# K and V of each context chunk: eight block products replaced by seven shared ones (Strassen, one level)

## The reference, cut to what matters

```
q = proj(layernorm(x), Wq, bq);  k = proj(ctx, Wk, bk);  v = proj(ctx, Wv, bv)   # [256|25088, 512] x [512, 512]
scores = q @ k.T / sqrt(64)         # per head of 64 columns, 2 sequence halves of the context
out = softmax(scores) @ v           # x + out goes on
```

## Time and profile before

| | us |
|---|---|
| median of 3 runs (1722.69 to 1724.3) | 1722.85 |
| profiled execution, its own time | 1723.75 |
| its span, first to last instruction | 1722.0 |
| PE busy / DVE / ACT / POOL in the span | 1661.5 / 1090.8 / 1095.7 / 365.8 |

### The profile page before, as it was taken

The page is one execution under the profiler, slowest core; times in us unless marked ns, Lnnn a source line. Parts: engine busy times, 40 slices in busy tenths (PEclk is TensorE's granted clock), DMA queues, the critical chain, the costliest instruction groups (busy, mean ns, idle before and its releaser), DMA issues.

```text
span 1722.0 us, 38963 instructions
## 1 busy us (share of the span) xinstructions
PE 1661.5 (96%) x14196; PEld 930.2 (54%) x14196; DVE 1090.8 (63%) x1559; ACT 1095.7 (64%) x2775; POOL 365.8 (21%) x500
## 2 busy tenths in 40 slices
PE   6999999999999999999999999999999587999998
PEld 3455555555555555555555555555555365777776
DVE  4666666666666666666666666666666556676765
ACT  3676676766766667666676666666666435555554
POOL 3222222222222222222222222322222100000000
PEclk9999999999999999999999999999999775999999
DMA  6466554555545555455554655545554470465551
GB/s 239 83 127 124 108 122 103 128 122 110 122 100 131 119 112 123 97 134 113 114 126 97 133 106 120 128 97 130 106 122 83 81 251 1 148 214 189 207 195 50
DMA packets 442396, 215.93 MB, mean 125 GB/s; under 512 B 416736, under 2 KB 422880, under 8 KB 435568
## 3 DMA queue, kind: packets, MB, share of 16 engines
q1 hardware_dynamic: 442064, 215.07, 51.6%
q10 hardware_dynamic: 288, 0.27, 0.1%
HBM read 111.96 MB, written 0.56 MB: 65 GB/s over the span
## 4 chain that ended last, share of the span: by engine, by line
PE 94%; DVE 2%; ACT 1%; DMA 1%; issue 1%; POOL 0%; SPq 0%; DVEq 0%; ACTq 0%; POOLq 0%
PE ps_proj L828 60%; PE ps_proj L948 9%; PE ps_s L845 9%; PE ps_o L864 8%; PE ps_o L971 4%; PE ps_s L904 1%; PE ps_proj L884 1%; PE ps_proj L915 1%; DVE wsp L655 1%; DMA ctx_f<-ctxt_dram 1%; PE ps_o L891 0%; PE ps_o L807 0%; ACT prob L390 0%; POOL ctx_s L306 0%; DVE cmax L584 0%
## 5 line engine op out<-in xcount | busy, mean ns | idle before, releaser
L828 PE MATMUL ps_proj<-ctx_s,wk_s 128*128 128x512 f16 x2352 | 542.1, 381 | 9.4 <-POOL ctx_s L306 9.4
L828 PE MATMUL ps_proj<-wv_s,ctx_s 128*128 128x512 f16 x2352 | 540.2, 379 | 0.0
L390 ACT ACTIVATE prob<-ps_s,nmax 128x256 f32<-128x256 f32 x784 | 360.5, 471 | 231.5 <-DVE nmax L591 231.5
L306 POOL TENSOR_TENSOR ctx_s<-ctx_f,ctx_s 128x512 f16<-128x512 f32 x196 | 230.6, 1177 | 908.8 <-ACT ctx_s L355 908.8
L828 PEld LDWEIGHTS ps_proj<-ctx_s,wk_s 128*128 128x128 f16 x2352 | 216.2, 98 | 264.7 <-issue 23.9
L828 PEld LDWEIGHTS ps_proj<-wv_s,ctx_s 128*128 128x128 f16 x2352 | 215.4, 98 | 252.7 <-issue 20.3
L573 DVE SCALAR_TENSOR_TENSOR k_s<-ps_proj,bk_s,k_s 128x512 f16<-128x512 f32 x196 | 147.1, 751 | 222.7 <-ACT k_s L362 222.7
L610 DVE SCALAR_TENSOR_TENSOR p_s<-prob,p_s 128x1024 f16<-128x1024 f32 x196 | 240.2, 1226 | 55.1 <-ACT p_s L401 55.1
L584 DVE TENSOR_REDUCE cmax<-ps_s 128x4 f32<-128x1024 f32 x196 | 239.1, 1220 | 25.7 <-PE ps_s L845 25.6
L576 DVE TENSOR_TENSOR v_s<-ps_proj,v_s 128x512 f16<-128x512 f32 x196 | 134.5, 686 | 186.5 <-ACT v_s L364 186.5
L401 ACT ACTIVATE p_s<-prob 128x1024 f16<-128x1024 f32 x196 | 210.4, 1073 | 0.1
(11 more groups left out here) (118 smaller groups left out, 904.1 us busy)
## 6 DMA issues: line engine op xcount, KB each, us to landing
ctx_f<-ctxt_dram SPq DMA_DIRECT2D x49, 1024.0 KB, 5.1
wst<-w_dram SPq DMA_DIRECT2D x96, 512.0 KB, 4.2
pt_s<-p_s SPq DMA_TRANSPOSE x392, 3.2
w_in_sb<-w_in_dram SPq DMA_DIRECT2D x1, 3072.0 KB, 11.6
tisa<-tisa_scores SPq DMA_DIRECT2D x3, 1024.0 KB, 14.1
w_f<-wk_dram SPq DMA_DIRECT2D x1, 1024.0 KB, 7.9
w_f<-wv_dram SPq DMA_DIRECT2D x1, 1024.0 KB, 11.9
w_f<-wq_dram SPq DMA_DIRECT2D x1, 1024.0 KB, 13.6
```

The lines of the kernel that those rows point to most:

```text
L306: pool.tensor_tensor(out=ctx_s[odd][1][:, t, :], in0=ctx_f[odd][:, t, :], in1=ctx_s[odd][0][:, t, :], op=ALU.subtract).then_inc(ctx_low, 1)
L390: ins = act.activation(prob[:, g % 2, (2 * b + r) * HC:(2 * b + r + 1) * HC], ps_s[:, b, r * HC:(r + 1) * HC], ACT.Exp, bias=nmax[odd][:, ...
L828: ins = pe.matmul(ps_proj[:, u % 4, :], lhsT, rhs, start=(t == 0 and n == 0), stop=(t == DT - 1 and n == 2))
```

## The change

With a chunk's context as a 2 x 2 of blocks b11, b12, b21, b22 (256 input features x 256 rows each) and the weight likewise, K and V each take seven block products (Winograd's form) in place of eight. The pieces are:

- Context: four sums t1 to t4 (fp32, 512 elements a partition each) on POOL, then high and low parts of seven blocks in place of four. ACT writes the high parts of three blocks (one instruction of 1024, one of 512 elements), POOL copies the high parts of the four sums (two of 1024) and writes all low parts (three of 1024, one of 512).
- Weights: the same sums once, at the start, for K on DVE and for V on POOL, with their high and low parts; chunk 0's low parts on DVE.
- PE: `unit` is 12 matmuls of 256 columns (before: 12 of 512), 14 units a chunk (before: 8). They are M1, M5, M6, M2, M7, M3, M4 for K (first half of a step, h = 0) and again for V (h = 1), laid around the scores of two groups and two weightings.
- Shared products are combined in PSUM: ACT copies M1's bank into a second one (`seed`), on which M6 accumulates; ACT copies M5 to SBUF (`copy_m5`); DVE adds it (`add_u4`, then `add_c22`). Four output blocks for K and four for V are then split as before (`block_highs` on ACT, `block_lows` on DVE).
- `step` has two halves instead of four groups. In it the high and low part of an odd group's probabilities go to the next half. The load of `w_in_sb` moves from the start to step 47, into memory that the context's buffers leave; `tisa_scores` and `project_q` change places at the start.

The core of the diff:

```
-            def project(c, odd, u):
...
+            def unit(k, odd, h, m):
+                w, x, role = m
+                g, first = 2 * k + h, isinstance(k, int) and k == 0
...
+                if m == M1:
+                    if h == 0 and not first:
+                        pe.wait_ge(ctx_low, DT * (k + 1))
+                    if not isinstance(k, int) or g >= 1:
+                        pe.wait_ge(block_low, 4 * g - 3)
+                elif m == M5:
+                        pe.wait_ge(block_low, 4 * g - 2)
+                elif m == M6:
+                    pe.wait_ge(seeded, g + 1)
+                elif m == M7:
+                    pe.wait_ge(u4_done, g + 1)
+                elif m == M4:
+                    pe.wait_ge(c22_done, g + 1)
+                for sub in range(2):
+                    for t in range(2):
+                        for i, (a, b) in enumerate(THREE):
...
+            def step(c, odd):                                 # PE
+                for h in range(2):
+                    for half, before, between, behind in ((0, (M1,), (M5, M6), (M2, M7)), (1, (), (M3,), (M4,))):
+                        g = 2 * h + half
+                        units(*before)
+                        if exists(c, 0):
+                            scores(c, g, odd)
+                        units(*between)
+                        vc, vg = back(c, g, PV_LAG)
+                        if exists(vc, 0):
+                            weigh(vc, vg, odd if g >= PV_LAG else 1 - odd)
+                        units(*behind)
...
+            def step(c, odd):                                 # ACT
+                for h in range(2):
+                    if exists(c, h):
+                        block_highs(c + h, 1 - h, C21, odd if h == 0 else 1 - odd)
+                    if exists(c, 1):
+                        seed(c + 1, h)
+                    pc, pg = back(c, 2 * h, 1)
+                    if exists(pc, 0):
+                        p_highs(pc, pg)
...
+                    if exists(c, 1):
+                        copy_m5(c + 1, h)
+                    if exists(c, 0):
+                        exps(c, 2 * h, odd)
                     if exists(c, 2):
+                        ctx_highs(c + 2, odd, h)
...
+                        p_highs(c, 2 * h)
                     if exists(c, 1):
+                        for which in (C11, C22, C12):
+                            block_highs(c + 1, h, which, 1 - odd)
                     if exists(c, 0):
+                        exps(c, 2 * h + 1, odd)
...
             def step(c, odd):                                 # DVE
+                for h in range(2):
+                    if exists(c, h):
+                        block_lows(c + h, 1 - h, C21, odd if h == 0 else 1 - odd)
                     if exists(c, 0):
+                        maxima(c, 2 * h, odd)
...
+                        p_lows(pc, pg)
                     if exists(c, 1):
+                        add_u4(c + 1, h)
+                    if exists(c, -1):
+                        add_o(c - 1, h)
                     if exists(c, 0):
+                        p_lows(c, 2 * h)
+                    if exists(c, 1):
+                        add_c22(c + 1, h)
+                    if exists(c, 0):
+                        maxima(c, 2 * h + 1, odd)
+                        step_max(c, h, odd)
+                    if exists(c, 1):
+                        for which in (C11, C22, C12):
+                            block_lows(c + 1, h, which, 1 - odd)
...
+            def add_c22(k, h):
+
+                g = 2 * k + h
+                dve.wait_ge(unit_done, UNITS * g + 5)
+                dve.tensor_tensor(half_bank(bank(h, 3)), half_bank(bank(h, 1)), m5_f[:, :, :], ALU.add).then_inc(c22_done, 1)
...
-            def ctx_lows(k, odd, pieces):
+            def ctx_sums(k, odd):                             # POOL
+                pool.wait_ge(ctx_loaded[odd], 8 * k + (16 - 8 * odd))
+                    pool.wait_ge(ctx_low, DT * k)
+                pool.tensor_tensor(out=t1, in0=b12, in1=b11, op=ALU.subtract).then_inc(t_sum, 1)
+                pool.tensor_tensor(out=t3, in0=b22, in1=b12, op=ALU.subtract).then_inc(t_sum, 1)
+                pool.tensor_tensor(out=t2, in0=b22, in1=t1, op=ALU.subtract).then_inc(t_sum, 1)
+                pool.tensor_tensor(out=t4, in0=t2, in1=b21, op=ALU.subtract).then_inc(t_sum, 1)
+            def ctx_parts(k, odd, half):                      # POOL, step c: ctx_parts(c + 2, odd, h), then rescale
+                high, low = ctx_s[odd]
+                if half == 0:
+                    ctx_sums(k, odd)
+                    if after(k, -2):
+                        pool.wait_ge(unit_done, 2 * UNITS * (k - 1))
+                    pool.wait_ge(t_sum, 4 * k + 4)
+                    pool.wait_ge(ctx_high, 2 * k + 1)
+                    pool.tensor_tensor(out=low[:, 0:2, :, :].rearrange("p b t k -> p (b t) k"),
+                                       in0=ctx_f[odd][:, :, 0:QUARTER],
+                                       in1=high[:, 0:2, :, :].rearrange("p b t k -> p (b t) k"),
+                                       op=ALU.subtract).then_inc(ctx_low, 1)
+                    pool.tensor_copy(high[:, 3:5, :, :], t_f[:, 0:2, :, :]).then_inc(t_high, 1)
+                else:
+                    pool.tensor_copy(high[:, 5:7, :, :], t_f[:, 2:4, :, :]).then_inc(t_high, 1)
+                    pool.wait_ge(ctx_high, 2 * k + 2)
+                    pool.tensor_tensor(out=low[:, 2, :, :], in0=ctx_f[odd][:, 2:4, QUARTER:CH], in1=high[:, 2, :, :],
+                                       op=ALU.subtract).then_inc(ctx_low, 1)
+                    for n in range(2):
+                        pool.wait_ge(t_high, 2 * k + n + 1)
+                        pool.tensor_tensor(out=low[:, 3 + 2 * n:5 + 2 * n, :, :], in0=t_f[:, 2 * n:2 * n + 2, :, :],
+                                           in1=high[:, 3 + 2 * n:5 + 2 * n, :, :], op=ALU.subtract).then_inc(ctx_low, 1)
```

More of the change, by code:

```diff
@@ L41 @@
 PV_LAG = 2
+UNITS = 7
+QUARTER = 256
 EPS = 1e-5
@@ L249, in step @@
                         load_chunk(c + 3, 1 - odd)
+                    if isinstance(c, int) and c == NCH - 2 and g == 0:
+                        sp.wait_ge(ctx_low, DT * NCH)
+                        sp.dma_start(w_in_sb[:, :, :], w_in).then_inc(w_in_loaded, 16)
             cross_steps(sp, step)
@@ L409, in _ @@
+            weight_highs(1)
+            weight_sum_highs(1)
             for g in range(2):
@@ L790, in _ @@
             pe.wait_ge(ident_ready, 1)
+            for n in (1, 2):
+                for t in range(DT):
+                    pe.matmul(ps_proj[:, n, t * P:(t + 1) * P], ident[:, :], ident[:, :], start=(t == 0), stop=(t == DT - 1),
+                              skip_group_check=True)
             turn(0)
@@ new lines, in scores @@
+            def scores(c, g, odd):
+                if g == 0:
+                    pe.wait_ge(block_low, 8 * c + 4)
+                if isinstance(c, int) and c == 0 and g == 0:
+                    pe.wait_ge(q_ready, 1)
+                if g >= 1 or after(c, -1):
+                    pe.wait_ge(exp_done, NG * c + g)
+                for r in range(2):
+                    for n, (a, b) in enumerate(THREE):
+                        for head in range(2):
+                            rows = slice(DK * head, DK * head + DK)
+                            ins = pe.matmul(ps_s[:, head, r * HC:(r + 1) * HC], q_s[a][rows, g, r * P:(r + 1) * P],
+                                            k_s[odd][b][rows, g, r * HC:(r + 1) * HC], start=(n == 0), stop=(n == 2))
+                ins.then_inc(s_done, 1)
@@ new lines, in step, with units @@
+            def step(c, odd):
+                for h in range(2):
+                    def units(*which):
+                        for m in which:
+                            if exists(c, 1):
+                                unit(c + 1, 1 - odd, h, m)
+                    for half, before, between, behind in ((0, (M1,), (M5, M6), (M2, M7)), (1, (), (M3,), (M4,))):
[8 more added lines that the diff above has]
+                        units(*behind)
+                    if isinstance(c, int) and c == -1 and h == 0:
+                        project_q()
+                    if isinstance(c, int) and c == -1 and h == 1:
```

450 lines of the change are left out of this document (273 added, 177 removed).

## The result

The changed kernel takes 1764.11 us (median of 4, 1762.92 to 1764.98), the kernel before 1722.96 on the same chip: ratio 1.0237, 95% interval 1.0219 to 1.0255. The span of the profiled execution is 1762.1 us against 1722.0.

The account below looks back on a forecast made before the run. PE bounded the kernel before; after the change, waits at the SBUF port shared by POOL and DVE would decide. 1723.75 + 47 x 0.6 - 2.8 + 15 = 1764 us, range 1690 to 1800.

Parts of the forecast that it names:

- PE's part: PE's work: a unit takes 1.31 us, a half step 12.11, a chunk 24.2; 133 us gained if PE never waits.
- rival 1: The port between POOL and DVE costs nothing that PE sees: 24.2 us a chunk, 1606 us; chance 0.09.
- POOL's instructions: Lengths on POOL: sums 1.04 us each, 1024-element low parts 2.1, 1024-element copies 1.1.
- The V half: Second half of a step: DVE's p low, nmax and dmax wait for POOL, so it takes 13.9 us, not 12.11.
- the prediction's bound of 13.1: The V half can't fall much below 13.1 us while POOL's chain of instructions stands.
- The K half: First half of a step: p low waits 1.2 us for POOL's 1024-element low part; the half takes 13.7 us.
- The 48 steps: Steps with projections: +0.6 us a chunk (27.6 against 26.98) for 47, and -2.8 in the last, at 24.2.
- The start: Before the loop: DVE and POOL alternate until about 28, chunk 0's scores start at 67 instead of 50.55: +15 us.
- Rival 2: POOL's 1024-element instructions are shorter than 2.1 us, pays from 26.7 a chunk down; 1698 us at its bound; chance 0.19.
- Rival 3: The port queue grows, POOL's lows end after M1's due time, PE waits: 29 us a chunk, 1830 us; chance 0.10.
- The signs: In the profile: PE busy about 88%, idle 1.5 to 1.8 us before M1; nmax 0.5, dmax 1.1, p low 1.8.
- POOL's upper bound: POOL's busy time per chunk: put at 16.8 us, up to 19.4.

Follow-up runs that it names:

- e5: The changed kernel with, from chunk 2 on, GpSimd's context work cut to 4 elements a row block, and the rescaling of o_acc too; 1625.98 us, ratio 0.9435.
- e2: The changed kernel with dmax issued behind the low parts of C11 on DVE's queue; 1747.35 us, ratio 1.0140.
- e10: e9 with w_in's load issued one step later; 1647.7 us, ratio 0.9564.
- e9: e6 plus reordered start (V's weight low parts, residual bias, tisa arguments behind K's units) and GpSimd's 1024-element low parts each as two of 512; 1650.02 us, ratio 0.9581.
- e11: The changed kernel with only each of GpSimd's 1024-element low parts as two instructions of 512; 1725.68 us, ratio 1.0011.
- e6: e2 plus GpSimd's low parts of sums first in V half, probabilities' high part before context's on ACT, U4 added before odd group's p low; 1666.15 us.
- e8: The kernel before the change, with two unused 1024-element GpSimd subtractions behind each context low part; 2039.21 us, ratio 1.1833.

## Why the prediction was right, step by step

- **PE's part.** A unit was put at 1.31 and a half at 12.11. In e5, where PE waits for nothing, a half is 12.30. A unit in front of scores takes 1.41, a tenth over, and there are two in a half: 0.2 a half, 19 us over the loop. The forecast did not feel it since PE wasn't the bound, but rival 1 was that much too low (1606; e5 has 1626).
- **POOL's instructions.** 1024-element low parts 2.12 to 2.16 for 2.1, copies 1.03 for 1.1. The sums were mis-sized: 1.27 for 1.04. L321, from which 1.04 came, reads one of its inputs by broadcast; that this is the reason is not shown.
- **The V half.** Walked as 13.9, measured 13.71. p low starts 7.62 into the half (7.65 in the walk), `dmax` ends 13.06 (13.35) behind POOL's second low part, for which it waits. The order of meetings is the predicted one, `nmax` at the seam included: it ends 10.97 into the half, walked 11.1. e2 shows what the place of `dmax` is worth by itself: 0.5 of the 1.4 us by which the half is over PE's 12.31. Behind it stands GpSimd's own last low part, as the prediction's bound of 13.1 has it (13.18 in e2).
- **The K half.** 13.7, measured 13.78. Sums end 6.6 into the half, not 4.9 (0.9 of it by their length, the rest by a p low of DVE, 704.07 to 705.28, which the fourth meets); the excess was slack, since the low part there waits for ACT in any case. p low ends 10.6, walked 10.4.
- **The 48 steps.** +0.6 for 47 and -2.8 in the last: 25.4. Measured 25.0, as 47 x 0.54 less 0.2 in the last. The last step is a miss of its own: it takes 26.8, not 24.2. In its V half (14.47) the weighting waits for a transpose behind w_in's 3 MB load, which took 10.7 us to land and was put at 0 with 1 either way; e10 has 2.3 us less than e9 by moving the load alone. So 25.4 came out near by luck: the 47 steps gave 25.2 where 28.2 were forecast, and the last gave back 0.2 where it was to give 2.8.

```profile
1384.49 0.87 PE L1133 MATMUL ps_o<-v_s,pt_s 128*128 128x64 f16 x24 [1.91 <-DMA pt_s<-p_s]
```

- **The start.** +15, measured +17.1. The alternation of DVE and POOL until 28 came as walked:

```profile
13.93 2.28 DVE L719 TENSOR_TENSOR ctx_s<-ctx_f,ctx_s 128x1024 f16<-128x1024 f32 x1
15.09 2.24 POOL L352 TENSOR_TENSOR t_f<-ctx_f,t_f 128x512 f32<-128x512 f32 x1
16.13 2.28 DVE L710 SCALAR_TENSOR_TENSOR wk_s<-sum_f,wk_s 128x1024 f16<-128x1024 f32 x1
```

  Each waits for the other's end and then takes its turn, 2.2 us for a pair. What followed was too short: the seed is done at 38.6, not 35, since GpSimd's sums for chunk 1 meet the small instructions of DVE there; one of 2 elements a row took 1.18 us:

```profile
29.75 1.26 POOL L350 TENSOR_TENSOR t_f<-ctx_f 128x512 f32<-128x512 f32 x1
29.85 1.18 DVE L737 TENSOR_TENSOR bk_d<-bk_s 128x2 f32<-128x2 f32 x1
```

- **The rivals.** Rival 1 (the port costs nothing) fell by the 1764 itself, and by e5: without most of GpSimd's work the time is 1626. Rival 2's condition, shorter 1024-element instructions, was not met at 2.13; cut in two (e11) they give a chunk of 26.76, where that rival begins to pay, and 1726, not the 1698 of its bound. Rival 3 (PE waits for `ctx_low`) does not show in the changed kernel, where GpSimd's last low part ends 0.68 us before M1. It came in e2, at 0.70 a chunk, and in e11.
- **The signs.** PE busy 89% for 88. The means came out lower than named: `nmax` 0.35 for 0.5, `dmax` 1.07 for 1.1, p low 1.51 for 1.8, and PE is idle for 1.23 and 1.02 before M1, not 1.5 to 1.8. The p low of the odd group in the K half got in front of GpSimd's fourth sum and did not wait; and PE's own work was put 0.2 a half too low.
- **Slips in the prediction's sums.** POOL's upper bound is 20.2, not 19.4 (the low parts' 0.8 is left out); 47 x 0.28 is 13.2, not 12.2; a chunk of 28.1 with a start of +22 gives 1796, not 1792. The forecast rests on none of them.
- **Luck.** The sum added 40.4 us and the spans show 40.1 (41.2 between the medians), with terms off by 2 to 3 us: besides the two in the 48 steps, the start's +2 is set off by -2.3 behind the loop, which was put at 0. The mechanism was right by itself; a sum within 1 us was not to be had from terms of this size. Why the last chunk's attention is that much shorter was not tried.

## What to carry to other kernels

Where GpSimd and VectorE both work from SBUF, price a new GpSimd instruction by who meets it, not by its busy time: in this kernel the smallest VectorE operation with both inputs in SBUF waited for its whole rest. Write long GpSimd instructions in pieces and put them where VectorE reads PSUM or is idle; with the same arithmetic this kernel went from 2.4% slower to 4.4% faster by order and cutting alone. Before an instruction is moved back to spare one wait, look at what is behind it: in e6 the transposes behind p low cost nearly what the move gained. And walk both engines' queues in time ahead of such a change: the totals (20.1 and 16.8 of 24.2 us here) say nothing of it.

## What the runs showed of the hardware

- An 8-element `dmax` took 2.06 us behind a GpSimd instruction of 1024 elements, 1.08 behind one of 512 (e11), 0.17 alone.
- Beside a GpSimd busy at nothing (e8) `nmax`, both inputs in SBUF, has a mean of 1550 ns for 194; the maxima, which read PSUM, keep 1217 for 1220, and V's low part, one input in PSUM, 685 for 686.
- The two engines take turns: between two GpSimd instructions issued back to back a waiting VectorE instruction gets in (e8: `nmax` ends 711.58 within a pair that runs 709.43 to 713.77), and when both have work, each takes every second place (start of the changed kernel).
- GpSimd, two float32 inputs of 512 elements: 1.27 us; float32 less float16 of 512: 1.16, of 1024: 2.13; float32 to float16 copy of 1024: 1.03, so a copy costs half of what a subtraction does.
- Beside a 3 MB load PE waited 1.91 us (changed kernel) and 4.25 us (e9) for small transposing DMAs of another purpose; with the load one step later (e10) that wait is gone and the step 4.7 us shorter.
